# Shared network's 704 hidden units cut as five blocks of 128 and one of 64, with gate and value columns of the last block in one product group

## What is computed

```
xn = layernorm(x)
yg = xn @ shared_gw.T                 # 1408 columns: 704 values y, then 704 gates g
shared = (silu(g) * y) @ shared_dw.T  # 704 -> 512
scores = sigmoid(xn @ gate_w.T); top 2 of 8 experts per row, weights normalised
out = sum over the two experts of w_e * ((silu(xn @ gate_e.T) * (xn @ up_e.T)) @ down_e.T)
x = x + tanh(g_ffn) * (shared + out)
```

## Time and profile before

| what | value |
|---|---|
| median of 3 runs | 594.91 us (593.76 to 595.9) |
| profiled execution | 595.18 us, its span 593.4 us |
| mean granted TensorE clock | 0.925 |
| PE busy | 507.4 us, 86% of the span |
| DVE busy | 343.6 us, 58% |
| ACT busy | 262.0 us, 44% |
| POOL busy | 232.2 us, 39% |
| up products, L845 | 2 x 288, busy 80.2 and 79.7 us |
| down products, L862 | 2 x 144, busy 35.7 and 34.9 us |
| experts' products, L984, L985, L1004 | busy 140.7, 140.7, 82.1 us |

### The profile page before, as it was taken

One profiled execution on the slowest core, in us unless ns is written; L12 is line 12 of the kernel. 1 busy time (PEld: TensorE's weight loads), 2 busy tenths in 40 slices (PEclk: granted clock), 3 DMA queues, 4 the chain that ended last, 5 costly groups with the idle time before them and its releaser, 6 DMA issues.

```text
span 593.4 us, 11085 instructions
## 1 busy us (share of the span) xinstructions
PE 507.4 (86%) x3169; PEld 289.1 (49%) x3170; DVE 343.6 (58%) x708; ACT 262.0 (44%) x473; POOL 232.2 (39%) x226
## 2 busy tenths in 40 slices
PE   2402589979998999879998899999999999999992
PEld 0100354434444454344464466666666666666660
DVE  0589758787868786977974377533333333333330
ACT  1696588646774579433231156322222222222221
POOL 1147735462446434550233034343343343443422
PEclk9655769989998999997999799999999999999997
DMA  3235293205611472034004489545445445445333
GB/s 113 97 91 173 80 305 108 57 30 182 250 42 36 138 275 57 21 106 147 1 1 159 149 230 242 123 77 95 79 75 95 78 78 96 74 77 97 74 43 46
DMA packets 32050, 63.75 MB, mean 107 GB/s; under 512 B 4049, under 2 KB 4305, under 8 KB 32017
## 3 DMA queue, kind: packets, MB, share of 16 engines
q1 hardware_dynamic: 23280, 42.89, 22.1%
q0 software_dynamic: 8736, 20.45, 18.9%
HBM read 41.05 MB, written 22.28 MB: 107 GB/s over the span
## 4 chain that ended last, share of the span: by engine, by line
PE 58%; DVE 17%; ACT 9%; issue 7%; DMA 5%; POOL 2%; SPq 1%; DVEq 1%; POOLq 0%; ACTq 0%
PE py L1004 12%; PE pg L984 12%; PE pu L985 12%; PE pg L845 4%; PE pu L845 4%; PE pt_bank L804 3%; DVE w L1178 3%; DVE pa L1137 3%; DVE w L1108 2%; PE pa L994 2%; PE py L862 2%; ACT w L613 2%; ACT w L619 2%; PE pu L862 2%; DVE w L1141 1%
## 5 line engine op out<-in xcount | busy, mean ns | idle before, releaser
L984 PE MATMUL pg<-w,x_t 128*128 x468 | 140.7, 313 | 0.0
L985 PE MATMUL pu<-w,x_t 128*128 x468 | 140.7, 313 | 0.0
L541 POOL DMA_INDIRECT out<-rows,idx x39 | 61.8, 1584 | 142.3 <-ACT rows L744 134.6
L1004 PE MATMUL py<-w,work 128*128 x351 | 82.1, 379 | 0.8 <-DVE work L1435 0.8
L845 PE MATMUL pg<-w 128*128 128x512 f16 (+1 forms) x288 | 80.2, 389 | 1.9 <-DVE work L1231 1.9
L845 PE MATMUL pu<-w 128*128 128x512 f16 (+1 forms) x288 | 79.7, 387 | 0.0
L734 ACT ACTIVATE work<-pg 128x352 f32<-128x352 f32 x39 | 18.0, 463 | 135.2 <-PE pu L985 135.2
L580 ACT ACTIVATE w<-stage 128x544 f16<-128x544 f32 (+1 forms) x80 | 50.7, 647 | 34.8 <-DMA stage<-in_weights 34.6
L488 POOL TENSOR_TENSOR w<-stage,w 128x544 f16<-128x544 f32 (+1 forms) x43 | 54.0, 1264 | 27.4 <-ACT stage L584 25.5
L494 POOL TENSOR_TENSOR work<-work 128x512 f16<-128x512 f32 (+1 forms) x24 | 29.0, 1209 | 81.9 <-ACT work L649 81.9
L1424 DVE SCALAR_TENSOR_TENSOR work<-pu,work 128x352 f32<-128x352 f32 x39 | 20.5, 524 | 62.6 <-ACT work L734 62.5
(11 more groups left out here) (189 smaller groups left out, 760.8 us busy)
## 6 DMA issues: line engine op xcount, KB each, us to landing
stage<-in_weights SPq DMA_DIRECT2D x80, 272.0 KB, 3.1
w<-in_x SPq DMA_DIRECT2D x4, 1024.0 KB, 6.6
out<-w SPq DMA_DIRECT2D x16, 256.0 KB, 2.8
xn_rows<-w SPq DMA_DIRECT2D x16, 256.0 KB, 5.3
out<-rows SPq DMA_DIRECT2D x13, 256.0 KB, 3.2
rows<-out SPq DMA_DIRECT2D x12, 256.0 KB, 3.0
w<-in_ctx_t SPq DMA_DIRECT2D x4, 256.0 KB, 3.4
out<-rows,idx POOLq DMA_INDIRECT x39, 4.7
```

The source lines that it names most:

```text
L541: pool.indirect_dma_start(out=out, out_offset=bass.IndirectOffsetOnAxis(ap=idx[:, t:t + 1], axis=0), in_=rows[:, t % 2, :], in_offset=None ...
L984: pe.matmul(pg[p][:, 0:H], lhs, w[:, item, half, at:at + H], start=begin, stop=end)
L985: mm = pe.matmul(pu[p][:, 0:H], lhs, w[:, item, half, at + H:at + 2 * H], start=begin, stop=end)
L1004: mm = pe.matmul(py[:, :], hid_t[:, p, part * JC + j, :], w[:, item, half, at:at + C], start=(j, part, half) == (0, 0, 0), stop=(j, part) ...
```

## The change

The 704 units are taken as one row of blocks: five of 128 and one of 64 (`MIXED` = 5, `REST` = 64). For the last one the 64 gate columns and the 64 value columns stand side by side in one block of 128 weight columns, so that one group of 12 products gives the gate in partitions 0 to 63 of bank `pg[1]` and the value in partitions 64 to 127. The silu reads the first 64 partitions and writes the other 64 of `hb`; the product and the high part stay in those; the low part is written to partitions 0 to 63 of the same `hid_tb` block that holds the high part in 64 to 127. The 64 down rows are stored twice, one below the other. One product over all 128 partitions then gives (high + low) x high weights, and a second over the upper 64 gives high x low weights: 5 x 3 + 2 = 17 products for a row tile. The host lays the shared weights out anew (`shared_group` tells in which item and column a block stands); their size and their loading stay. POOL waits for its operation before the low part of unit 5 and for that low part's own end after it.

```diff
+UPS = HALVES * JC
+SHARED = HALVES * H
+MIXED = UPS - 1
+REST = SHARED - MIXED * P
+def shared_group(group, k):
+    if group < 2 * MIXED:
+        return group // MIXED, (group % MIXED * KC + k) * P
+    return k * HALVES // KC, (MIXED * KC + k % (KC // HALVES)) * P
...
             def shared_low(b, u):
-                q, m = b * UPS + u, PIECES[u][2]
+                q = b * UPS + u
                 after(pool, hhi_sb, q + 1)
-                pool.tensor_tensor(hid_tb[0:m, u, 1, :], hb[0:m, u % 2, :], hid_tb[0:m, u, 0, :], ALU.subtract).then_inc(hlo_sb, 1)
+                if u == MIXED:
+                    after(pool, hlo_sb, q)
+                    pool.tensor_tensor(hid_tb[0:REST, u, 0, :], hb[REST:, u % 2, :], hid_tb[REST:, u, 0, :],
+                                       ALU.subtract).then_inc(hlo_sb, 1)
+                    after(pool, hlo_sb, q + 1)
+                    return
+                pool.tensor_tensor(hid_tb[:, u, 1, :], hb[:, u % 2, :], hid_tb[:, u, 0, :], ALU.subtract).then_inc(hlo_sb, 1)
...
             def shared_silu(b, u):
-                q, m = b * UPS + u, PIECES[u][2]
+                q, at = b * UPS + u, REST if u == MIXED else 0
                 after(act, up_mm, q + 1)
                 after(act, hlo_sb, q - 1)
-                act.activation(hb[0:m, u % 2, :], pg[u % 2][0:m, :], ACT.Silu, scale=UP_UNSCALE).then_inc(sil_sb, 1)
+                act.activation(hb[at:, u % 2, :], pg[u % 2][0:P - at, :], ACT.Silu, scale=UP_UNSCALE).then_inc(sil_sb, 1)
...
                 for k in ks:
-                    for bank_, at in ((pg[u % 2], k * 2 * H + off), (pu[u % 2], k * 2 * H + H + off)):
+                    banks = (pg[u % 2],) if u == MIXED else (pg[u % 2], pu[u % 2])
+                    for n, bank_ in enumerate(banks):
+                        half, at = shared_group(2 * u + n, k)
                         for part, xpart in ((0, 0), (0, 1), (1, 0)):
-                            mm = pe.matmul(bank_[0:m, :], w[:, half, part, at:at + m], x_tb[:, xpart * KC + k, :],
+                            mm = pe.matmul(bank_[:, :], w[:, half, part, at:at + P], x_tb[:, xpart * KC + k, :],
                                            start=(k, part, xpart) == (0, 0, 0), stop=(k, part) == (KC - 1, 1))
...
-                    at = UP_W + off // P * C
+                    half, at, cols = u // JC, UP_W + u % JC * C, slice(i * P, (i + 1) * P)
+                    if u == MIXED:
+                        pe.matmul(bank_[:, :], hid_tb[:, u, 0, cols], w[:, half, 0, at:at + C], start=False, stop=False)
+                        mm = pe.matmul(bank_[:, :], hid_tb[REST:, u, 0, cols], w[REST:, half, 1, at:at + C], start=False, stop=True)
+                        continue
...
             def shared_hidden(b, u):
-                q, m = b * UPS + u, PIECES[u][2]
+                q, at = b * UPS + u, REST if u == MIXED else 0
+                values = pg if u == MIXED else pu
```

More of the change, by code:

```diff
@@ L14 @@
 JC = HP // P
-PIECES = [(h, j * P, min(P, H - j * P)) for h in range(HALVES) for j in range(JC)]
-UPS = len(PIECES)
+UPS = HALVES * JC
+SHARED = HALVES * H
+MIXED = UPS - 1
+REST = SHARED - MIXED * P
 SLOTS_STEP = 4
@@ L639, in shared_silu @@
             def shared_silu(b, u):
-                q, m = b * UPS + u, PIECES[u][2]
+                q, at = b * UPS + u, REST if u == MIXED else 0
                 after(act, up_mm, q + 1)
                 after(act, hlo_sb, q - 1)
-                act.activation(hb[0:m, u % 2, :], pg[u % 2][0:m, :], ACT.Silu, scale=UP_UNSCALE).then_inc(sil_sb, 1)
+                act.activation(hb[at:, u % 2, :], pg[u % 2][0:P - at, :], ACT.Silu, scale=UP_UNSCALE).then_inc(sil_sb, 1)
             def shared_high(b, u):
-                q, m = b * UPS + u, PIECES[u][2]
+                q, at = b * UPS + u, REST if u == MIXED else 0
                 after(act, hid_sb, q + 1)
                 after(act, down_mm, b * TPB)
-                act.activation(hid_tb[0:m, u, 0, :], hb[0:m, u % 2, :], ACT.Copy).then_inc(hhi_sb, 1)
+                act.activation(hid_tb[at:, u, 0, :], hb[at:, u % 2, :], ACT.Copy).then_inc(hhi_sb, 1)
             def scores_and_rows(b, more, pieces=()):
@@ L834, in shared_up @@
             def shared_up(b, u, beside=None, ks=range(KC)):
-                half, off, m = PIECES[u]
                 if u == 1 and beside is not None:
@@ L856, in shared_down @@
                 for u in pieces:
-                    half, off, m = PIECES[u]
                     after(pe, hhi_sb, b * UPS + u + 1)
                     after(pe, hlo_sb, b * UPS + u + 1)
-                    at = UP_W + off // P * C
+                    half, at, cols = u // JC, UP_W + u % JC * C, slice(i * P, (i + 1) * P)
[3 more added lines that the diff above has]
+                        continue
                     for part, wpart in ((0, 0), (0, 1), (1, 0)):
-                        mm = pe.matmul(bank_[:, :], hid_tb[0:m, u, part, i * P:(i + 1) * P],
-                                       w[0:m, half, wpart, at:at + C],
-                                       start=(u, part, wpart) == (0, 0, 0), stop=(u, part) == (UPS - 1, 1))
+                        pe.matmul(bank_[:, :], hid_tb[:, u, part, cols], w[:, half, wpart, at:at + C],
+                                  start=(u, part, wpart) == (0, 0, 0), stop=False)
                 if UPS - 1 in pieces:
@@ L1227, in shared_hidden @@
             def shared_hidden(b, u):
-                q, m = b * UPS + u, PIECES[u][2]
+                q, at = b * UPS + u, REST if u == MIXED else 0
+                values = pg if u == MIXED else pu
                 after(dve, sil_sb, q + 1)
                 after(dve, up_mm, q + 1)
-                dve.scalar_tensor_tensor(out=hb[0:m, u % 2, :], in0=pu[u % 2][0:m, :], scalar=UP_UNSCALE * H_SCALE,
-                                         in1=hb[0:m, u % 2, :], op0=ALU.mult, op1=ALU.mult).then_inc(hid_sb, 1)
+                dve.scalar_tensor_tensor(out=hb[at:, u % 2, :], in0=values[u % 2][at:, :], scalar=UP_UNSCALE * H_SCALE,
+                                         in1=hb[at:, u % 2, :], op0=ALU.mult, op1=ALU.mult).then_inc(hid_sb, 1)
             def shared_rows(b, i):
@@ L1488, with shared_items @@
     up_w, down_w = np.asarray(L0_ffn_up_w), np.asarray(L0_ffn_down_w)
-    S = HALVES * H
-    items = [item(gw[S + h * H:S + (h + 1) * H], gw[h * H:(h + 1) * H], dw[:, h * H:(h + 1) * H]) for h in range(HALVES)]
+    def shared_items():
+        gate, value, down = gw[SHARED:], gw[:SHARED], dw.T
+        groups = []
+        for u in range(UPS):
+            of = [m[u * P:u * P + P].T for m in (gate, value)]
+            groups += [np.concatenate(of, axis=1)] if u == MIXED else of
+        downs = [down[u * P:(u + 1) * P] for u in range(MIXED)] + [np.concatenate([down[MIXED * P:]] * 2)]
+        both = np.zeros((HALVES, P, ITEM_W), np.float32)
+        for n, group in enumerate(groups):
+            for k in range(KC):
+                half, at = shared_group(n, k)
+                both[half, :, at:at + P] = group[k * P:(k + 1) * P]
+        for u in range(UPS):
+            both[u // JC, :, UP_W + u % JC * C:UP_W + (u % JC + 1) * C] = downs[u]
+        return list(both)
+    items = shared_items()
     items += [item(up_w[e, :H], up_w[e, H:], down_w[e]) for e in range(EXPERTS)]
```

## The result

The changed kernel took 589.89 us (median of 4 runs, 588.87 to 590.2) against 594.35 us, a ratio of 0.9918 with a 95% interval of 0.9894 to 0.9942. With the later runs of the same two kernels, timed beside the experiments, the medians are 589.89 us (10 runs) and 594.53 us (94 runs), the means 589.92 +- 0.36 and 594.29 +- 0.17 (an error behind +- is one standard error): 4.4 us less, where 3.2 were forecast. One run of an experiment, 596.53 us, was in the chip's slower state and is left out of the means.

A forecast was written before the change was run, and what follows sets the result against it. PE's products were taken as time only where PE is waited for, with DVE's chain the path elsewhere in the passes. -2.59 - 0.22 - 0.22 - 0.22 + 0.07 = -3.2 us from 594.91 gave 591.7 us, range 589.9 to 594.4.

The forecast's parts named there:

- Unit 5 in the tail: In batch 3's shared network, 12 fewer up products in unit 5 lie on the path: -2.59 us.
- Unit 5 in the passes: In the shared networks of batches 0 to 2, 12 fewer products lie before DVE's missed-row count: 0 us gained.
- 17 down products: One product less per down tile: -0.22 us each for tail tiles 0 and 3 and pass 1's tile 2, otherwise 0.
- up to 0.6 us: Pass 1's turning of attention, slow before, might run fast if the clock is back up in time: up to 0.6 us.
- POOL's low part across partitions: Unit 5's new low part on POOL takes 1.2 us (bounds 0.6 and 2.4); cost 0, at worst 1.5 us.
- The threshold pair under the low part of unit 4: DVE's threshold pair takes 1.79 us in each pass: -0.47, +0.49 and +0.05 us in passes 0, 1, 2, sum +0.07.
- the small operation behind the pair: In pass 2, DVE's operation after the threshold pair loses 0.44 us (0.59 there, 0.15 in pass 0), offsetting the pair's 0.49.
- The clock: Forecast case (0.78): 8 slow products more or fewer at the tail's two slow starts, 1.7 us either way.
- The first rival: PE's longer idle times in the passes lower its clock through all 22 down products before the turning: 597.3 us, chance 0.04.
- a swallowed gain: Slot operands, unit 5's low part or weight DMAs cancel the tail's 2.8 us: about 594.7 us, chance 0.08.
- engines beside: POOL's low part across partitions at its bound (+1.5 us) or port blocks in the passes (+1.4): 593.2 us, chance 0.10.

## Why the prediction was right and wrong

- *Unit 5 in the tail, -2.59 us:* right. Unit 5 takes 2.59 us in the trace, the slot steps follow at once, and neither the slot operands nor unit 5's low part held PE up. Twelve products put back there cost 3.6 +- 0.6 us, not clearly more than that.
- *Unit 5 in the passes, 0:* right for the path. The idle times before the count are 4.5, 3.5 and 3.1 us (forecast: about 5.0, 3.1 and 3.1; the shorter and longer threshold pairs make the difference). For the clock it is open: the longer wait draws the low clock to products nobody waits for, and away from the turning of attention, in the first trace but not in pass 1 of the second; twelve products put back cost 1.5 +- 0.5 us, which the traces don't place in the passes. The prediction had this for pass 1 ("up to 0.6 us") and left it out of the sum.
- *17 down products, -0.22 us for a tile on the path, three of them:* wrong. The term took 0.216 us for every product. The 64-row product and the one before it take 0.31 us each, so a tile costs 3.86 us instead of 3.89, and the slot steps behind tile 0 take another 0.1. Tile 0 with them gave +0.07, tile 3 -0.02. Pass 1 gained nothing either: PE then waits 0.72 us for DVE at the turning of rows. That DVE had waited for PE there in the earlier trace rows was due to the slow turning before it: where that ran at the full clock, the stretch from the turning to the up units took 19.0 us in both kernels.
- *POOL's low part across partitions, 0:* right, 1.15 us (1.24 in the mean of four).
- *The threshold pair under the low part of unit 4:* right in size, 1.79 us in all three passes. But the sum of the three came out at +0.3 us, not +0.07: from the pair to the turning of pass 0 it took 0.4 us less, and from the up units to the turnings of passes 1 and 2 0.5 and 0.16 us more. The prediction had counted on the small operation behind the pair to give back 0.44 us in pass 2; it did become short (0.15 us), but the turning did not gain all of it.
- *The clock:* this step of the forecast failed. It was taken as a spread of 1.7 us either way about zero, as if the change could not shift its mean. The kernel before has its low clock in the tail in both traces, 5.3 us for twelve products; the changed one had it there in part of them and shorter. With the waits filled the difference of the two kernels falls from 4.4 +- 0.4 to 2.0 +- 0.7 us. The first rival's direction (longer waits, lower clock, more time) did not come about: twelve products at 4.4 us fit into the cover.
- *The rivals* of a swallowed gain and of engines beside are out. The first of them was worked out slightly too high: 2.8 us taken back from 591.7 us give 594.5, not 594.7.

With terms as read from the traces, the path gives -2.6 (unit 5) +0.1 (tiles) +0.3 (the pair: -0.4, +0.5, +0.2), some -2.2 us, and what is left of the 4.4 us, some -2 us, goes to the clock. That the forecast came as near as it did is in part luck: the path was taken 1 us too large and the clock 2 us too small. The clock's share rests on the filled kernels and on few traces; why it falls less before down tile 3 is open.

## What to carry to other kernels

Shortening PE's work ahead of a wait can change where its clock falls: ask, for each wait of PE as long as those here (2.3 to 4.5 us), what runs behind it, and whether somebody waits for that. Where it is waited for, products without a use in the wait are cheap: 46 of them made the kernel before 3.4 us faster. Look at a second trace before a slow or a fast stretch is put down to a change; here stretches that the change did not touch moved by 3 to 4 us between executions. A saved product is priced by the spacing of rows like it in the trace; a product of another height (64 rows among 128) has to be priced by itself, and widening it to the full height was free here.

## What the runs showed of the hardware

- A product over partitions 64 to 127 among products over all 128: its weight load came 0.42 us behind the one before it, just ahead of its own product, and the next load was late as well; 0.31 us from product to product instead of 0.216. Widened to 128 partitions it took 0.21 us, and the stage from the slot steps to the table 10.93 us for 11.23. Products over the first 96 partitions, in the kernel before, showed no such thing (18 in 3.89 us).
- Waits of PE of 2.3 to 2.9 us before down tile 3, each behind an idle time of 0.2 to 1.2 us and eight short products: the granted clock fell from 2.4 to 1.2 GHz in or after seven of ten (unfilled), and in none of seven filled with ten products. The same program differs from one execution to the next.
- A GpSimd operation from partitions 64 to 127 to partitions 0 to 63, 64 x 512, takes 1.15 us when nothing hinders it, as one of 128 partitions does.
